# Feature operand with one head per 64 partitions, feature tiles in pairs of row strips

## The reference

```
h = layernorm(x) * (1 + ca) + sa
q, k, v = split(h @ W_attn + b_attn);  q, k scaled by 1/4
phi(u) = exp(u @ omega - |u|^2 / 2) / sqrt(128)          # omega is 16 x 128
y = (phi(q) . cumsum(phi(k) v)) / (phi(q) . cumsum(phi(k)) + eps)    # causal, per head
x = x + ga * (y @ W_proj + b_proj)
h = layernorm(x) * (1 + cb) + sb
w = the top 2 of 4 softmax gates of h @ Wg.T + bg
out = sum_e w_e * relu(h @ Wi.T + (h @ A_e.T) @ B_e.T) @ Wo.T       # F = 1024, rank 4
x = x + gb * out
```

## Time and profile before

| | |
|---|---|
| three runs | 836.02, 839.67, 840.61 us (median 839.67) |
| profiled execution | 835.22 us, of which the span from the first to the last instruction is 833.4 us |
| mean granted TensorE clock | 0.984 |
| busy share of the span | PE 92%, PEld 72%, DVE 66%, ACT 49%, POOL 6% |
| chain that ended last | PE 73%, DVE 14%, DMA 7%, issue 3%, ACT 2% |
| DMA | 65.37 MB, 78 GB/s over the span |

### The profile page before, as it was taken

The page is one execution under the profiler, slowest core; times in us unless marked ns, Lnnn a source line. Parts: engine busy times, 40 slices in busy tenths (PEclk is TensorE's granted clock), DMA queues, the critical chain, the costliest instruction groups (busy, mean ns, idle before and its releaser), DMA issues.

```text
span 833.4 us, 16957 instructions
## 1 busy us (share of the span) xinstructions
PE 765.5 (92%) x6138; PEld 603.4 (72%) x6138; DVE 546.9 (66%) x1289; ACT 410.9 (49%) x758; POOL 47.0 (6%) x62
## 2 busy tenths in 40 slices
PE   2989998999899999999999998999999998999596
PEld 2767767876698766977678765987678776887366
DVE  5546666776667775776666766677656766665456
ACT  2365545564456444654455544564446543555122
POOL 1101000010001000010000100010000100010000
PEclk9979999999999999999999999999999999999989
DMA  8680072203702064111722037020731017110000
GB/s 271 149 196 2 24 207 57 76 0 94 189 0 75 0 194 89 43 32 42 195 45 75 0 103 180 0 75 0 202 81 57 18 50 200 33 52 1 1 1 26
DMA packets 46540, 65.37 MB, mean 78 GB/s; under 512 B 8716, under 2 KB 22840, under 8 KB 46392
## 3 DMA queue, kind: packets, MB, share of 16 engines
q1 hardware_dynamic: 46520, 65.10, 29.0%
HBM read 39.87 MB, written 25.17 MB: 78 GB/s over the span
## 4 chain that ended last, share of the span: by engine, by line
PE 73%; DVE 14%; DMA 7%; issue 3%; ACT 2%; SPq 1%; DVEq 0%; POOL 0%; ACTq 0%
PE pa L513 11%; PE prod L528 7%; DMA qk_parts<-qk_l 6%; PE ring L492 6%; PE pa L379 5%; PE pa L381 4%; PE pa L380 4%; PE prod L547 4%; PE pa L619 4%; PE ring L379 4%; PE ring L497 3%; PE ring L380 3%; PE ring L381 3%; PE prod L513 2%; PE ring L695 2%
## 5 line engine op out<-in xcount | busy, mean ns | idle before, releaser
L513 PE MATMUL pa<-phq,phkT 128*128 128x128 f32 x896 | 115.1, 276 | 0.0
L513 PEld LDWEIGHTS pa<-phq,phkT 128*128 128x128 f32 x896 | 107.8, 191 | 2.3 <-issue 1.6
L820 ACT ACTIVATE phq<-ring 128x512 f32<-128x512 f32 x96 | 58.9, 614 | 90.6 <-PE ring L492 89.7
L1077 DVE TENSOR_TENSOR am_phk<-pa,const 128x512 f32<-128x512 f32 x112 | 74.2, 685 | 32.0 <-PE pa L513 32.0
L1230 DVE SCALAR_TENSOR_TENSOR am_phk<-ring,am_phk 128x512 f32<-128x512 f32 x64 | 44.2, 691 | 55.4 <-PE ring L695 55.4
L379 PE MATMUL pa<-wo_r,qk_r 128*128 128x256 f32 x256 | 72.1, 282 | 0.6 <-DVE qk_l L1235 0.6
L381 PE MATMUL pa<-wo_l,qk_r 128*128 128x256 f32 x256 | 72.1, 282 | 0.0
L380 PE MATMUL pa<-wo_r,qk_l 128*128 128x256 f32 x256 | 71.8, 281 | 0.0
L882 ACT ACTIVATE qk_r<-phq 128x512 fp32r<-128x512 f32 x64 | 40.5, 632 | 63.3 <-DVE phq L1239 62.8
L528 PE MATMUL prod<-am_phk,v_ones 128*32 128x256 f32 x1024 | 61.9, 382 | 4.6 <-DVE tg L1108 4.6
L379 PE MATMUL ring<-h_r,wi_r 128*128 128x512 f32 x128 | 57.7, 451 | 3.6 <-DVE am_phk L1230 2.9
(11 more groups left out here) (189 smaller groups left out, 1566.2 us busy)
## 6 DMA issues: line engine op xcount, KB each, us to landing
xq<-qk_parts SPq DMA_DIRECT2D x48, 512.0 KB
qk_parts<-qk_r SPq DMA_DIRECT2D x32, 256.0 KB, 3.3
qk_parts<-qk_l SPq DMA_DIRECT2D x32, 256.0 KB, 3.6
tok<-in_L_attn_x SPq DMA_DIRECT2D x8, 512.0 KB, 4.6
xr<-in_L_attn_x SPq DMA_DIRECT2D x8, 512.0 KB, 3.7
out_x<-tg SPq DMA_DIRECT2D x16, 256.0 KB, 2.2
norm_parts<-norm_r SPq DMA_DIRECT2D x16, 128.0 KB, 3.5
norm_parts<-norm_l SPq DMA_DIRECT2D x16, 128.0 KB, 5.1
```

The costliest lines, as they stand in the source:

```text
L513: mm = pe.matmul(score_bank(q, a)[:, tt], phkT[:, q % 2, a, tt], phq[:, q // 2 % 2, 2 * (q % 2) + a, tt], start=True, stop=True)
L820: act.activation(dst, src, ACT.Exp).then_inc(exp_done.sem, 1)
L1077: dve.tensor_tensor(am[:, 2 * (q % 2) + a, :].rearrange("p (c t) -> p c t", c=NT), score_bank(q, a)[:].rearrange("p (c t) -> p c t", c=NT) ...
```

## The change

`xq` and `omega_x` are laid out anew: head a of a pair has partitions 64a to 64a+49, with 16 rows times three copies (row r, copy c at 3r + c) and two norm rows. Rows 50 to 63 are zero, and XROWS goes from 100 to 114. Tiles 0 to 3 are reordered so that tiles 0, 1 are the two heads' q and tiles 2, 3 the two heads' k, and each takes the 50 rows of its own head only: rows 0 to 49 or 64 to 113. The DRAM buffer holds the three copies, so q and k are stored in three DMAs for each quarter, and read back in two of 48 rows for each half. `AHEAD` puts two tiles at steps 0, 2, 6 and 8. `low` moves to a part of `am_phk`, and the wait for `qk_out` moves to ACT's first write of `g_r`. POOL clears partitions 32 to 63 of `xq` once.

```diff
-XROWS = 3 * PAIR_ROWS + 4
+HEAD_ROWS = 64
+NORM_ROW = 3 * DH
+KROWS = NORM_ROW + 2
+XROWS = HEAD_ROWS + KROWS
...
-AHEAD = {0: 1, 1: 1, 2: 2, 3: 1, 5: 1, 6: 1, 7: 1, 8: 1, 9: 2, 10: 1}
+AHEAD = {0: 2, 2: 2, 3: 1, 4: 1, 6: 2, 8: 2, 9: 1, 10: 1}
...
-        xq = sb("xq", [XROWS, 2, 2, HALF, T], F32R)
+        xq = sb("xq", [2 * HEAD_ROWS, 2, 2, HALF, T], F32R)
...
-        g_r, g_l, low = qk_r[:, 0:3], qk_l[:, 0:3], qk_r[0:LROWS, 3]
+        g_r, g_l = qk_r[:, 0:3], qk_l[:, 0:3]
+        low = am_phk[0:LROWS, 2, 0]
...
                 for k, part in enumerate((om_r, om_l, om_r)):
-                    row = k * PAIR_ROWS + a * DH
-                    move(omega_x[row:row + DH, a * M:(a + 1) * M], part[:]).then_inc(om_moved.sem, 16)
-            move(omega_x[3 * PAIR_ROWS:XROWS, :], nrow_r[:]).then_inc(om_moved.sem, 16)
+                    rows = slice(a * HEAD_ROWS + k, a * HEAD_ROWS + NORM_ROW, 3)
+                    move(omega_x[rows, a * M:(a + 1) * M], part[:]).then_inc(om_moved.sem, 16)
+                row = a * HEAD_ROWS + NORM_ROW
+                move(omega_x[row:row + 2, :], nrow_r[2 * a:2 * a + 2, :]).then_inc(om_moved.sem, 16)
...
-                    for part, src in enumerate((qk_r, qk_l)):
-                        sp.dma_start(parts_out[part, j], src[:, j, :].bitcast(F32)).then_inc(qk_out[j // 2].sem, 16)
+                    for copy, src in enumerate((qk_r, qk_r, qk_l)):
+                        sp.dma_start(parts_out[j, :, copy], src[:, j, :].bitcast(F32)).then_inc(qk_out[j // 2].sem, 16)
...
-                    for copy, part in enumerate((0, 0, 1)):
-                        src = parts_out[part, 2 * half:2 * half + 2].rearrange("k (i r) t -> r (k i) t", r=PAIR_ROWS)
-                        sp.dma_start(xq[copy * PAIR_ROWS:(copy + 1) * PAIR_ROWS, half]
+                    for a in range(2):
+                        src = parts_out[2 * half:2 * half + 2].rearrange("k (i a r) c t -> a (r c) (k i) t", a=2, r=DH)[a]
+                        sp.dma_start(xq[a * HEAD_ROWS:a * HEAD_ROWS + NORM_ROW, half]
...
+            sp.wait_ge(set_pool.sem, 4)
             front_moves(0)
...
                     if k < 4:
-                        mm = pe.matmul(dst[:], omega_x[:, k // 2 * M:(k // 2 + 1) * M], xq[:, p // HALF, k % 2, p % HALF, :],
-                                       start=True, stop=True)
+                        rows = slice(k % 2 * HEAD_ROWS, k % 2 * HEAD_ROWS + KROWS)
+                        mm = pe.matmul(dst[:], omega_x[rows, k % 2 * M:(k % 2 + 1) * M],
+                                       xq[rows, p // HALF, k // 2, p % HALF, :], start=True, stop=True)
...
                 if q:
-                    wait(pe, exp_done, n, q * TILES + 2 * a + 2)
+                    wait(pe, exp_done, n, q * TILES + a + 3)
...
-                if front_next:
-                    for signal in qk_out:
-                        wait(act, signal, n + 1, signal.per)
-                act.activation(low, ring[2][0:LROWS, :], ACT.Copy).then_inc(low_high.sem, 1)
+                act.activation(low.bitcast(F32R), ring[2][0:LROWS, :], ACT.Copy).then_inc(low_high.sem, 1)
...
                         wait(act, g_sum, n, k + 1)
+                        if k == 0 and front_next:
+                            for signal in qk_out:
+                                wait(act, signal, n + 1, signal.per)
...
                 pool.memset(mk2[:], 0.0).then_inc(set_pool.sem, 1)
+                pool.wait_ge(set_pool.sem, 3)
+                pool.memset(xq[32:HEAD_ROWS].bitcast(F32), 0.0).then_inc(set_pool.sem, 1)
                 pool.wait_ge(ld_late.sem, 16 * LATE_LOADS)
...
-    parts_out = nc.dram_tensor("qk_parts", (2, 4, P, T), F32, kind="Internal").ap()
+    parts_out = nc.dram_tensor("qk_parts", (4, P, 3, T), F32, kind="Internal").ap()
```

More of the change, by code:

```diff
@@ L233, in build @@
         norm_mm, norm_full, norm_split = sig("norm_mm", 2), sig("norm_full", 2), sig("norm_split", 2)
-        qk_out = [sig(name, 4 * 16) for name in ("qk0_out", "qk1_out")]
+        qk_out = [sig(name, 6 * 16) for name in ("qk0_out", "qk1_out")]
         norm_out = [sig(name, 2 * 16) for name in ("norm0_out", "norm1_out")]
-        moved = [sig(name, 7 * 16) for name in ("moved0", "moved1")]
+        moved = [sig(name, 6 * 16) for name in ("moved0", "moved1")]
         v_ps, v_done = sig("v_ps", 2), sig("v_done", 2)
@@ L349, in front_moves @@
                         for a in range(2):
-                            row = 3 * PAIR_ROWS + 2 * part + a
+                            row = a * HEAD_ROWS + NORM_ROW + part
                             src = norms_out[part, rows].rearrange("(k r) t -> k r t", r=VA)[:, a * GROUP:(a + 1) * GROUP]
@@ L468, in setup_late @@
                 mm.then_inc(late_pe.sem, 1)
-                pe.wait_ge(set_pool.sem, 9)
+                pe.wait_ge(set_pool.sem, 10)
                 pe.wait_ge(late_vec.sem, 3)
@@ L496, in features @@
                             t = (2 * (k - 4) + c) * P
-                            mm = pe.matmul(dst[:, c * 2 * M:(c + 1) * 2 * M], xq[:, p // HALF, 1, p % HALF, t:t + P], omega_x[:],
+                            mm = pe.matmul(dst[:, c * 2 * M:(c + 1) * 2 * M], xq[0:XROWS, p // HALF, 1, p % HALF, t:t + P], omega_x[:],
                                            start=True, stop=True)
@@ L730, in _ @@
             setup_late()
-            pe.wait_ge(om_moved.sem, 16 * 7)
+            pe.wait_ge(om_moved.sem, 16 * 8)
             pe.nop().then_inc(tok_free.sem, 1)
@@ L817, in features @@
                     else:
-                        dst = (phq[:, slot, 2 * (q % 2) + k // 2, :], phkT[:, q % 2, k // 2, :])[k % 2]
+                        dst = (phq[:, slot, 2 * (q % 2) + k % 2, :], phkT[:, q % 2, k % 2, :])[k // 2]
                         src = proj_bank(tile)[:]
@@ L1221, in mask_low @@
                     wait(dve, mask_ps, n, q + 1)
-                    dve.tensor_tensor(dst, low.bitcast(F32), src[0:LROWS],
+                    dve.tensor_tensor(dst, low, src[0:LROWS],
                                       ALU.mult).then_inc(low_masked.sem, 1)
@@ L1256, in ffn_rest @@
                 wait(dve, low_high, n, 1)
-                dve.tensor_tensor(low[64:96, :], lg[64:96], low[64:96, :].bitcast(F32),
-                                  ALU.subtract).then_inc(low_split.sem, 1)
+                dve.tensor_tensor(low[64:96, :].bitcast(F32R), lg[64:96], low[64:96, :], ALU.subtract).then_inc(low_split.sem, 1)
                 router(n)
@@ L1312, in setup @@
                 pool.memset(mk2[:], 0.0).then_inc(set_pool.sem, 1)
+                pool.wait_ge(set_pool.sem, 3)
+                pool.memset(xq[32:HEAD_ROWS].bitcast(F32), 0.0).then_inc(set_pool.sem, 1)
                 pool.wait_ge(ld_late.sem, 16 * LATE_LOADS)
-                pool.wait_ge(set_pool.sem, 3)
+                pool.wait_ge(set_pool.sem, 4)
                 for half, mk in enumerate((mk1, mk2)):
@@ L1381, in constants @@
         for a in range(2):
-            rows[2 * part + a, a * M:(a + 1) * M] = -0.5
+            rows[2 * a + part, a * M:(a + 1) * M] = -0.5
     return {"consts": np.ascontiguousarray(consts), "norm_rows": rows}
```

## The result

| | before | after |
|---|---|---|
| median | 839.24 us (836.02 to 842.61, 13 runs) | 843.43 us (840.74 to 846.59, 13 runs) |
| ratio | | 1.005, 95% interval 1.003 to 1.0069 |
| profiled execution, its span | 835.2, 833.4 | 844.0, 842.2 |
| first scores of the block after the setup | 55.79 | 62.25 |
| the seven blocks of the loop | 678.9 | 677.0 |

The account below looks back on a forecast made before the run. PE's stream was taken to bound the kernel. Terms -11.6 - 2 + 1.5 + 2.4 = -9.7 us on a span of 833.4 gave 823.7, or 825.5 for the execution; held against the median, 830. Range 819 to 841.

Parts of the forecast that it names:

- Part 1: Steady blocks: `low` leaves `qk_r`, so ACT's copy and DVE's router start 2.4 us earlier; 1.65 us a block, -11.6 us.
- the path of 6.10 us behind L651: In each block: from L651 to the first low-rank product, 6.10 us as in the last block, instead of 7.75.
- -2 for the clock: Steady blocks: a shorter PE hole lets most lower-clock blocks go; -2 us, bounds 0 and -3.
- The cover of part 1: Norms' store before DVE's L1222: lands at 317.8 to 319.0, needed at 319.0; no wait, at worst +3.5 us.
- The rival named after the norms: Steady blocks: L1222 waits 1 us for norms behind 1 MB more; part 1 gives 0.65 a block, 837; chance 0.10.
- Part 3: Setup: POOL's memset of about 7.0 us blocks DVE's work on the attention weights until it ends; +2.4 us.
- the bound I had put away as a rival: Setup: the memset blocks all of it, transposes and modulation too; +6 instead of +2.4, 833.5; chance 0.13.
- Part 2: Feature matmuls in paired row strips: attend -0.3, experts half of +0.9; +0.2 a block, +1.5 us, bounds -6 and +10.
- attend ends at DVE: Attend: PE's strip groups run while DVE works and PE then waits for it; at most 0.6 us a block.
- the rival with 0.20: Attend and experts: strips overlap and changing them is nearly free; -5.6 us instead of +1.5, 823; chance 0.20.
- no block at 0.98: Steady blocks: the sign for the clock, no block's mean granted clock at 0.98, where three of the first seven had it.

Follow-up runs that it names:

- e3_low: Kernel before with only the new place of `low` and the later wait for `qk_out`: 824.19 us, ratio 0.982.
- e4: Kernel before with a third, never read store of `qk_r` for each quarter: 852.84 us, ratio 1.0138.
- e6: Kernel before with the `low` part, three stores a quarter, and 96 rows on partitions 0 to 95 read in three DMAs of 32: 825.93 us, ratio 0.9853.
- e2: Changed kernel with the second half's norms stored from ACT's DMA queue in the loop: 835.48 us, ratio 0.9943.
- e5: Same kernel as e6, but the 96 rows are read in two DMAs of 48 partitions for each half: 829.64 us, ratio 0.9894.
- e7: Changed kernel with ACT clearing `xq[32:64]` and the second half's norms stored from ACT's queue: 832.54 us, ratio 0.995.
- e1: Changed kernel with partitions 32 to 63 of `xq` cleared by ACT and not by POOL: 842.13 us, ratio 1.0038.
- e14: e7 without strips (whole tiles), with DVE's attend gates and ACT's exps halved, leaving work out: 827.47 us, ratio 0.9831.
- e13: e7 with strips kept and DVE's attend gates and ACT's exps halved, leaving work out: 818.83 us, ratio 0.9734.

## Why the prediction failed, point by point

1. **Part 1, the wait at `low`: right, in mechanism and in size.** The router moves as said, and the path of 6.10 us behind L651 is 6.19 in e3_low. Alone the step gives 12.6 us in the seven blocks of the profiles, against the -11.6 and -2 for the clock that were forecast, and 15 us by the medians.
2. **The cover of part 1: the step that failed.** "So the norms land at 317.8 to 319.0 ... I take no wait." I had counted the third store's 0.5 MB a half (e4 confirms its size, 1.4 us), and then, in the part on the setup: "the reads of `xq` keep their bytes in four DMAs instead of six", at nothing. The bytes are the same, the rate is not: about 140 GB/s instead of 197. That is 3.3 us more for each half ahead of the norms (11.2 instead of 7.9), on top of the 1.4 for the third store, and past a margin that already ended at the 319.0 where L1222 needed them. From 6.9 us at worst the landing goes to 11.2. The third store alone doesn't make the norms late: e6 has it too, with reads at the old rate, and no wait. The wait is 10.3 us in six blocks, and removing it gives about 8 us (e2). The rival named after the norms was the right one for the steady blocks, with 10% and with the wrong reason (more bytes).
3. **Part 3, the setup: +2.4 taken, +6.5 measured.** The memset's length was right (7.0, 6.95). Where it hits was not: L1010 was caught by it, so transposes and modulation went with it; that was the bound I had put away as a rival. The rival has the size of the whole loss nearly right (+6), but by luck, since the memset isn't the bulk of it. The first block starts at 55.93 in e3, at 58.01 in e6 (three stores in the new order of rows), at 58.88 in e5 (reads of 48 rows, 0 to 95), at 60.78 in e7 (from partitions 0 and 64, and one more omega move) and at 62.01 in e2 (with the memset): steps of 2.1, 0.9, 1.9 and 1.2. Only their sum is firm. The nine kernels with e7's setup (e1, e7 to e14) start anywhere from 59.92 to 61.26, so a step of 0.9 or 1.2 between two profiles is no more than that spread; and the third store by itself (e4) starts at 56.21, so 1.7 of the first 2.1 us came with the new order of rows and not with the bytes, which no run takes apart further. The reads are the firmer part: the chain's last wait for `xq` is 8.78 us in e6, 9.91 in e5 and 10.97 in e7. Stores and reads had a cover in the setup, DVE's split of the FFN's weights until 46.57, and the longer ones outlast it; I had looked at the queue only for the steady block. On the shared port pair, the Trainium skill (SBUF — State Buffer, Who interferes with whom) says that the loser fully blocks; the pass of 7.09 us, through only when the memset is, agrees.
4. **Part 2, the strips: mis-sized (+0.5 a block with the table, e7 against e3; +0.2 taken), within its bounds.** In attend -0.1 (taken -0.3), in the FFN +0.3 for strips and +0.32 for the table (taken +0.5 for both). Leaving a strip group costs the 0.20 predicted in front of full-array work, 0.15 in front of L562, and nothing in front of column strips. A lone pair takes 0.43, and with the leaving 0.63, not 0.70; a group of four 0.66, and with the leaving 0.86, not 0.94. The two strips start together, not 0.11 apart, and behind other work a group shows no price of its own for entering. I had argued that attend ends at DVE and can't give more than 0.6. It gave 0.1, but not by that argument: with DVE lighter it still gave 0.07, and only with ACT lighter too 1.22. That ACT's exps pace the ring was not in the prediction. That two narrow tiles can run at once was the rival with 0.20, and it held for the products and not for the time. On mode changes, the Trainium skill (TensorEngine Tiling (Array Packing), Key Properties) has the drain; the trace shows 0.20 us on leaving for full-array work and none that can be seen on entering.
5. **The clock.** I forecast no block at 0.98. The profile of after has one steady block at 0.98 (97.9 us instead of 96.1), beside the first and the last; e3's blocks from the second on are even.

In numbers, for the median: low -15, reads and third store +8 in the norms and about +4.9 in the setup, memset +1.2 to +2, strips and table +4 (670.4 us in e7's seven blocks, 666.4 in e3's): +3 to +4, where +4.2 was measured.

**The best version** of all that do the whole work is e3_low, the part of the change that is about `low`, at 0.982 [0.9767, 0.9873] of before, from four runs. Everything else in the change costs; the strips gain only where ACT and DVE have room for what they save (e13).

## What to carry to other kernels

A layout change of a DMA's target is a change of its rate: before you write "same bytes", look at which partitions the rows fall on, and at what lands behind the transfer. A faster producer pays only where the consumer of its buffers is not at its own pace already; halve the consumers' work one after the other, with and without the change, and see which makes the difference appear. And single out the part of a change that removes a wait: here the part about `low` was worth 15 us and the rest took 19 back.

## What the runs showed of the hardware

- Reads from DRAM into 32 partitions run at 197 to 205 GB/s, into 48 partitions from 0 or 64 on at about 140, into 16 at about 120, and into 48 to 95 at 219 to 256, with the DMA engines shown as fully busy in all of them: the share of busy time doesn't tell a good layout from a bad one.
- Two matmuls of 50 rows and 512 columns in different row strips together take 0.33 us in a group, 0.43 as a lone pair, where one full matmul takes 0.23. Full-array work behind them pays 0.20 more, column strips nothing.
- A memset on POOL (10.15 to 17.10) held one DVE pass of 128x256 for 7.09 us instead of 0.40.
- With a ring of four banks whose exps come every 0.48 us, strip groups that could take 0.66 us take 0.88 to 1.06; with the exps halved they take 0.66.
